# Fourth attention: the high parts of keys and values written first in a step, the low parts one step later

## The reference

```python
def _L3_xattn_ref(x, context, ...):          # DIM 256, 16 heads of 64
    xn = _layernorm(x, ln_gamma, ln_beta)
    q = (xn @ w_q).reshape(B, SQ, NUM_HEADS, DIM_HEAD)
    kv = context @ w_kv
    k, v = jnp.split(kv, 2, axis=-1)
    scores = jnp.einsum('bqhd,bkhd->bhqk', q * SCALE, k)
    attn = jax.nn.softmax(scores, axis=-1)
    out = jnp.einsum('bhqk,bkhd->bqhd', attn, v).reshape(B, SQ, INNER)
    out = out @ w_out + b_out
    return out * jnp.tanh(gate[0])
x = x + jnp.tanh(g_xattn[3]) * _L3_xattn_ref(_layernorm(x, axis=-1), ctx_1024, ...)
```

## Time and profile before

| what | value |
|---|---|
| median of 3 runs | 3364.77 us (3358.12 to 3366.07) |
| the profiled execution's own time | 3355.87 us |
| its span, first to last instruction | 3354.1 us |
| mean granted clock of PE in the span | 0.878 |
| the fourth attention's loop over 8 batches | 2340 to 2852 us of the span |
| one of its middle batches | about 65.5 us |
| PE, DVE, ACT, POOL busy in the batch from 2468.7 us | 51.67, 42.10, 35.25, 29.00 us of 65.5 |

### The profile page before, as it was taken

The page is one execution under the profiler, slowest core; times in us unless marked ns, Lnnn a source line. Parts: engine busy times, 40 slices in busy tenths (PEclk is TensorE's granted clock), DMA queues, the critical chain, the costliest instruction groups (busy, mean ns, idle before and its releaser), DMA issues. The chain is left out here.

```text
span 3354.1 us, 56001 instructions
## 1 busy us (share of the span) xinstructions
PE 2648.1 (79%) x18080; PEld 2408.9 (72%) x18080; DVE 1604.1 (48%) x3706; ACT 1274.1 (38%) x3125; POOL 1249.8 (37%) x1203
## 2 busy tenths in 40 slices
PE   5673497499899999399968899992777777799893
PEld 4563386399888888289967788882777777688882
DVE  3665454566534444455522344334666666342232
ACT  3221143145443333154533344432555555433331
POOL 0012652743217560400046555133444443265313
PEclk9885698599889999699958999996888889799996
DMA  3031353200003341200026333141101010032212
GB/s 109 0 126 45 107 186 106 63 21 21 16 15 120 117 133 40 74 14 21 8 76 225 104 108 115 43 132 68 39 26 35 30 38 1 26 122 96 85 61 88
DMA packets 139056, 239.82 MB, mean 72 GB/s; under 512 B 17680, under 2 KB 89644, under 8 KB 136608
## 3 DMA queue, kind: packets, MB, share of 16 engines
q1 hardware_dynamic: 65536, 134.62, 12.9%
q10 hardware_dynamic: 59424, 64.09, 5.7%
q0 software_dynamic: 13824, 37.53, 3.6%
HBM read 162.35 MB, written 73.79 MB: 70 GB/s over the span
## 5 line engine op out<-in xcount | busy, mean ns | idle before, releaser
L562 ACT ACTIVATE moe_act<-moe_gu 128x256 f32<-128x256 f32 (+1 forms) x431 | 189.6, 440 | 617.6 <-PE moe_gu L95 617.6
L321 POOL TENSOR_TENSOR moe_wlo<-moe_raw,moe_whi 128x768 fp32r<-128x768 f32 (+1 forms) x170 | 340.6, 2004 | 36.6 <-issue 12.9
L853 DVE TENSOR_TENSOR moe_h<-moe_act,moe_gu 128x256 f32<-128x256 f32 x321 | 134.9, 420 | 372.7 <-ACT moe_act L562 355.9
L93 PE MATMUL moe_yp<-moe_whi,moe_hThi 128*128 (+1 forms) x926 | 291.9, 315 | 8.3 <-DVE moe_hTlo L869 8.1
L350 POOL DMA_INDIRECT moe_whi<-rows_y,moe_slot_r x144 | 139.0, 965 | 407.9 <-DMA rows_y<-moe_y 365.2
L93 PE MATMUL moe_gu<-moe_whi,moe_xThi 128*128 (+2 forms) x706 | 282.0, 399 | 0.1
L95 PE MATMUL moe_gu<-moe_whi,moe_xTlo 128*128 (+2 forms) x706 | 265.4, 376 | 0.0
L94 PE MATMUL moe_gu<-moe_wlo,moe_xThi 128*128 (+2 forms) x706 | 264.8, 375 | 0.0
L319 POOL CAST moe_whi<-moe_raw 128x768 fp32r<-128x768 f32 (+1 forms) x170 | 152.4, 896 | 300.8 <-DMA moe_raw<-in_moe_w 300.2
L95 PE MATMUL moe_yp<-moe_whi,moe_hTlo 128*128 (+1 forms) x926 | 261.6, 283 | 0.0
L94 PE MATMUL moe_yp<-moe_wlo,moe_hThi 128*128 (+1 forms) x926 | 261.3, 282 | 0.0
(11 more groups left out here) (491 smaller groups left out, 8157.2 us busy)
## 6 DMA issues: line engine op xcount, KB each, us to landing
moe_raw<-in_moe_w SPq DMA_DIRECT2D x118, 384.0 KB, 3.2
moe_raw<-in_moe_w SPq DMA_DIRECT2D x52, 512.0 KB, 4.5
moe_xr<-rows_x ACTq DMA_DIRECT2D x69, 256.0 KB, 2.8
rows_y<-moe_y ACTq DMA_DIRECT2D x69, 256.0 KB, 2.1
rows_x<-att_zeros SPq DMA_DIRECT2D x16, 512.0 KB, 6.2
kd<-moe_wlo ACTq DMA_DIRECT2D x32, 256.0 KB, 3.6
vd<-moe_wlo ACTq DMA_DIRECT2D x32, 256.0 KB, 3.8
w_wk_hi<-kd SPq DMA_DIRECT2D x8, 1024.0 KB, 4.8
```

The lines of the kernel that those rows point to most:

```text
L93: pe.matmul(out, lhs[0], rhs[0], start=first, stop=False, **kw)
L321: pool.tensor_tensor(lo_, cols, hi_.bitcast(F32), ALU.subtract).then_inc(w_done, 1)
L562: act.activation(act_sb[i % 2][:, :], gu[i % 2][:, 0:HC], func).then_inc(act_done, 1)
L853: v.tensor_tensor(h_sb[i % 2][:, :], act_sb[i % 2][:, :], gu[i % 2][:, HC:2 * HC], ALU.mult).then_inc(h_done, 1)
```

## The change

The two tables `K_AT` and `V_AT` become one table `HALVES`, one piece per step, in steps 3, 4, 6, 8, 10, 11, 13 and 14. On POOL the cast of a piece now stands first in its step, ahead of `normalize`. On DVE the low part of that piece stands one step later, in the place where it stood before (behind the inverse and the round).

```diff
-    K_AT = {7: 0, 9: 1, 11: 2, 14: 3}
-    V_AT = {2: (0, 2), 3: (0, 3), 10: (1, 0), 12: (1, 1)}
+    HALVES = {3: ("v", 0, 2), 4: ("v", 0, 3), 6: ("k", 1, 0), 8: ("k", 1, 1), 10: ("k", 1, 2), 11: ("v", 1, 0), 13: ("v", 1, 1), 14: ("k", 1, 3)}
...
+        def half_at(h, last):
+            kind, turn, part = HALVES.get(h, ("", 1, 0))
+            return ("", 0, 0) if last and turn else (kind, turn, part)
...
@@ DVE @@
-                        for kind, turn, part in halves_at(h, last):
-                            (k_lo if kind == "k" else v_lo)(i, lo, turn, part)
+                        kind, turn, part = half_at(h - 1, last)
+                        if kind == "k":
+                            k_lo(i, lo, turn, part)
+                        if kind == "v":
+                            v_lo(i, lo, turn, part)
...
@@ POOL @@
                     for h in range(H):
+                        kind, turn, part = half_at(h, last)
+                        if kind == "k":
+                            k_hi(i, lo, turn, part)
+                        if kind == "v":
+                            v_hi(i, lo, turn, part)
                         if not (last and h + 2 >= H):
                             normalize(i, lo, h + 2)
                         if h == 0 and not last:
                             norm(i, lo, 1)
-                        for kind, turn, part in halves_at(h, last):
-                            (k_hi if kind == "k" else v_hi)(i, lo, turn, part)
```

## The result

The changed kernel takes 3262.65 us against 3365.42 us (medians): ratio 0.9695, interval 0.9675 to 0.9716, 102.8 us less. One of the four runs of the changed kernel (3653.42 us at a granted clock of 0.70) was disturbed and is left out of the ratio. In a second set of five runs the same kernel took 3263.22 us, ratio 0.9686 (0.9653 to 0.9719).

A forecast was written before the change was run, and what follows sets the result against it. DVE's waits for POOL's casts were taken to set the pace, mainly from step 7 to step 1. Gains of 2.8 + 9.0 in six batches (70.8), 11 in the first and 2.4 in the last gave 84: 3280.5 us, range 3264 to 3322.

The forecast's parts named there:

- Stretch B: Middle batch from step 7's inverse to the next step 1's: 37.31 us falls to 27.5; gain taken as 9.0 us.
- a slow stretch of PE: From step 7 to the next step 1: a low PE clock makes PE late; 0.8 us taken off the gain.
- Stretch A: Middle batch from step 1's inverse to step 7's, 27.60 us before: gain 1.0 to 3.9 us, taken as 2.8.
- the direct row: DVE's step 3: the residual follows the inverse directly, 2.4 us earlier (1.71 wait, 0.69 low part).
- step 2: DVE's 6.05 us wait for a cast queued behind the norm; PE does the projection beside it, so little goes.
- all of its wait: PE's values of head 2 come up to 3.9 us earlier, with PE's clock higher behind a shorter pause.
- The two low parts in steps 4 and 5: On DVE, covered by its wait for the first query round's chain: cost nothing; without that cover 2 x 0.69 us.
- The collision: Low part and POOL's normalize both start behind the inverse and exclude each other; DVE first, POOL waits some 0.6 us.
- The rival that POOL wins: Each of six low parts from step 7 to 1 takes 1.75 us; 50 us gained, 3315 us; chance 0.13.
- The next wait takes over: PE's clock stays with its slow stretches, PE gives back about half its idle time; 55 us gained, 3310; chance 0.14.
- Only the name changes: Casts wait for PE's last reader and hold up normalize; only steps 1 to 7 gain, 20 us, 3345; chance 0.07.
- slower: PE's clock falls to 0.50 under the denser schedule; 13 us more a batch, 91 in all, 3456 us; chance 0.04.

The follow-up runs named there:

- a doubled operation: Changed kernel with every low part of the next batch's keys computed twice on DVE, four more operations a batch; 3300.7 us, ratio 0.9813 to the kernel before.
- the kernel with the cast first: Kernel before with only POOL's cast moved first in its step, old tables, DVE's low part in the same step; 3295.0 us, ratio 0.9787.
- the low part later: Kernel before with only DVE's low part one step later, old tables, POOL's cast still behind normalize; 3284.8 us, ratio 0.9758.
- the kernel with A alone changed: Kernel before with only the two values pieces of steps 2 and 3 handled as in the changed kernel; 3327.4 us, ratio 0.9896.
- its complement: Changed kernel with the two values pieces of steps 2 and 3 as before, the other six as changed; 3308.5 us, ratio 0.9812.
- removing the collision: Changed kernel with each low part moved ahead of the inverse of its step on DVE; 3276.5 us, ratio 0.9738 to the kernel before.

## Why the prediction was right in its mechanism and short in its size

**What bounds the loop: right, but for one pair of steps.** DVE's list sets the pace from step 7 to step 1. Its waits for casts went from 121.3 us to none, and a doubled operation there lengthened the pairs from 7 to 9, 9 to 11 and 15 to 1 by more than its own time. That PE's clock did not set it is seen in before as well: over the six batches the pair from 9 to 11 took 9.53 us at granted clocks from 0.74 to 0.86, that from 11 to 13 took 8.35 us at 0.75 to 0.89, and that from 13 to 15 took 7.50 us at 0.77 and at 1.00. Only the last pair answered to it (4.44 us at 1.00, 5.0 at 0.69, in two batches of six). So hardly any of B's gain came from the clock.

**Stretch B: right in size, in part by luck.** Forecast 9.0 us less, measured 9.3. Pair by pair (from step 7): 5.68, 5.67, 6.22, 5.82 and 4.81 us measured, 5.8, 5.8, 5.1, 5.8 and 5.04 forecast. Only the pair from 11 to 13 is off, by 1.1 us, and there the chain through PE ends last, at the output's low part:

```profile
2491.59 0.86 DVE L1479 TENSOR_TENSOR att_OT_lo<-att_o,att_OT_hi 64x256 fp32r<-64x256 f32 x2 [1.40 <-ACT att_OT_hi L1421]
```

I had taken 0.8 us off B for a slow stretch of PE. None came, the clock being 1.00 in every B of the changed kernel; this pair happened to fill the place.

**Stretch A: this step failed.** "Bounds for A: 2.4 - 1.4 = 1.0 to 3.9 us; I take 2.8". Measured are 5.04 us a batch, above the upper bound, and six times 2.24 are 13.4 of the 15.3 us by which the loop's gain of 99.5 exceeds the 84.2. Between inverses, as means over the six middle batches, in us:

| steps | before | changed | gain |
|---|---|---|---|
| 1 to 3 | 10.95 | 10.24 | 0.7 |
| 3 to 4 | 4.46 | 2.06 | 2.4 |
| 4 to 5 | 5.76 | 3.82 | 1.9 |
| 5 to 7 | 7.31 | 7.31 | 0 |

The 2.4 us of step 3, the direct row, came to the hundredth. Two terms were mis-sized. The larger is PE's clock, to which my 2.8 gave 0.4 us: in steps 4 to 5 it was worth 1.9. That it is the clock is shown by the kernel with the cast first, which has the same instructions in these steps as before: in three batches of one execution they took

```profile
2408.87:2412.63 3.76, 3.19 (x28) 2.95 (x26) 2.70 (x7) 2.79 (x10) 1.04 (x1) 1.00 0.57 240
2519.12:2524.44 5.32, 4.74 (x28) 4.50 (x26) 2.70 (x7) 2.79 (x10) 1.04 (x1) 0.68 0.41 169
2462.80:2468.98 6.18, 5.96 (x31) 5.72 (x30) 2.71 (x8) 2.79 (x10) 1.04 (x1) 0.59 0.35 146
```

against a batch of before and one of the changed kernel:

```profile
2551.60:2557.77 6.17, 5.96 (x31) 5.72 (x30) 2.70 (x7) 2.79 (x10) 1.04 (x1) 0.59 0.35 149
2463.78:2467.60 3.82, 3.18 (x28) 2.94 (x26) 3.78 (x8) 2.86 (x10) 1.04 (x1) 1.00 0.01 2
```

The smaller is step 2, of which the prediction said that PE does the projection beside DVE's wait, "so little goes", and which it took at nothing. Steps 1 to 3 gave 0.7 us. Two experiments bear this out: 10.95 us with the cast first, where the wait in step 2 stays, and 10.24 with the low part later, where it goes.

The slow stretch stood behind the pause of PE ahead of the values of head 2. That pause was 3.89 us in the batch that the prediction opened and 4.92 in the four longer ones, and is 1.41 in the changed kernel (of before, 19 matmul records in 3.70 us behind it; of the changed kernel, 34 in 4.10):

```profile
2485.00:2488.70 3.70, 3.58 (x19) 3.62 (x19) 2.18 (x6) 1.02 (x4) 1.04 (x1) 0.54 0.83 286
```

```profile
2462.80:2466.90 4.10, 4.10 (x34) 3.92 (x34) 4.10 (x8) 2.64 (x8) 1.80 (x3) 1.00 0.01 2
```

The transfer in the first of these rows (DMA share 0.83) is not what lowers the clock: the changed kernel has one at a share of 0.81 from 2470 to 2474 us, at a granted clock of 1.00. With the shorter pause the slow stretch did not come in any middle batch. I had mentioned the clock but put it inside "all of its wait", where it is a cost of its own behind the wait. And the batch that I cut, 27.60 us, was one of the two quick ones, with a clock of 0.93; the four others had 0.88 and 28.7 to 29.1 us:

```profile
2404.53:2433.23 28.70, 22.27 (x168) 21.63 (x167) 14.95 (x32) 13.72 (x43) 12.38 (x13) 0.88 0.10 38
```

**The two low parts in steps 4 and 5 at nothing: right.** They take 1.43 and 1.30 us there; the way from step 5 to 7 is 7.31 us with and without one, and moving the one of step 4 changed nothing.

**The rest of the sum.** B's 0.3 us too little make 1.7 us in six batches. The first batch gained 11.96 us (forecast 11), the last stretch A 4.26 (2.4), and what lies behind the last step 7 lost 2.8: it took 28.3 us at a granted clock of 0.88, against 25.5 at 1.00 before. That loss is chance and not the change: the repeated run of the changed kernel took 25.5 us there, and its loop 413.2. The 102.8 us between the medians and the 99.5 or 102.3 of the loops agree within the scatter of the unchanged phases.

**The collision: right in kind.** DVE is first, by 0.16 us and not 0.04, because the low part follows the inverse's start by 0.09 and not 0.2 us. POOL then loses 0.37 us, not 0.6. The rival that POOL wins holds only in steps 4 and 5. By the Trainium skill ("SBUF — State Buffer", section "SBUF: two separate sides") the one that starts first keeps the path and the other blocks. The 1.41 against 1.04 and the 1.53 against 0.67 us agree with it in kind; the added 0.37 us is less than the 0.51 for which the low part still ran.

**The other rivals.** "The next wait takes over" named PE's clock as what would hold back half of the gain; the clock went to 1.00 instead and gave some back. "Only the name changes" and "slower" fell with the same rows. Of the signs that I named, the "issue" wait (1.4) and the waits for exp (13.6, under 25) came as written; the batch was 51.6 us, not 53 to 55, and normalizes 1.41, not 1.6.

## What to carry to other kernels

When one engine's list has no idle time but for one releaser, cut its timeline at a repeated instruction, add up what is left without the waits, and the new period can come out close: B was forecast at 28.3 us and measured at 28.2, with one pair 1.1 us off and a spare term in its place. Then price what the removed pause does to PE behind it: if the granted clock in that stretch is below 1.00, compare two batches of the same code at different clocks, and take the mean over batches and not the one that was opened first. A producer whose operation stands behind a long one in its list can be mended from either side, by moving the producer up or the consumer one step down; here the one alone gave 75 and the other 85 us, of the 103 that both gave with the new table.

## What the runs showed of the hardware

The granted clock of PE went with the pauses of the stretch itself and changed within one batch: 1.00 in A and 0.86 to 0.91 in B of the kernel with A alone changed, and 0.88 to 0.94 in A and 1.00 in B of its complement. Pauses of 3.89 and 4.92 us were followed by a slow stretch in all six middle batches of before, those of 1.41 us in none of the changed kernel. In between, the length of the pause did not decide it: in the kernel with the low part later identical instructions with the same pause of 2.0 us took 24.0 us in two batches, at a clock of 1.00, and 25.3 to 25.5 in four, at 0.93. Where DVE set the pace, a clock of 0.74 in place of 0.86 cost nothing (9.53 us in the pair from 9 to 11); where PE's chain did, it added up to 2.4 us to 3.8 (6.18 against 3.76, with the cast first).

In the collision of a low part with normalize, with starts only 0.16 us apart, the second lost 0.37 us when it was POOL (1.41 against 1.04) and 0.74 when it was DVE (1.43 against 0.69). So their order at a common releaser is worth a look, even where, as here, removing the collision made nothing faster.
